# GpSimd's adds of the exponentials in a two-layer attention and expert kernel: one instruction per key tile instead of one per head

## What is computed

```python
# layer 0: x += 0.5 * moe0(layernorm(x)); x += attention0(layernorm(x)), 32 heads of 32; x += 0.5 * moe0(...)
# layer 1: attention1, 16 heads of 64; then routed experts with a capacity
qkv = data @ W_qkv + b_qkv
scores = jnp.einsum('nqhd,nkhd->nhqk', q, k)
attention = jax.nn.softmax(scores / jnp.sqrt(jnp.float32(HD)), axis=3)
out = jnp.einsum('nhql,nlhd->nqhd', attention, v).reshape(n, l, DIM)
return out @ W_out + b_out
# the router of layer 1: softmax over 8 experts, the two best, their weights divided by their sum
probs = jax.nn.softmax(xf @ router_w.T, axis=-1)
topw, topi = jax.lax.top_k(probs, K)
topw = topw / (topw.sum(-1, keepdims=True) + 1e-06)
```

## Time and profile before

| | us |
|---|---|
| median of three runs | 3018.5 |
| lowest and highest | 3016.71, 3020.96 |
| profiled execution: span from its first to its last instruction | 3025.9 |
| TensorE busy / share | 2770.4 / 92% |
| VectorE busy / share | 2107.9 / 70% |
| ScalarE busy / share | 1731.9 / 57% |
| GpSimd busy / share | 1752.1 / 58% |
| of it line 1982, 1152 adds | 1447.0 |

### The profile page before, as it was taken

How to read it: one execution, slowest core, us unless ns; L and a number is a source line. 1 busy time by engine, 2 the same in 40 slices (tenths; PEclk the granted TensorE clock), 3 DMA queues, 4 the chain that set the end, 5 groups by cost and what they waited for, 6 DMA issues and landing times. The chain is left out here.

```text
span 3025.9 us, 50008 instructions
## 1 busy us (share of the span) xinstructions
PE 2770.4 (92%) x17716; PEld 1938.1 (64%) x17716; DVE 2107.9 (70%) x4508; ACT 1731.9 (57%) x3340; POOL 1752.1 (58%) x1540
## 2 busy tenths in 40 slices
PE   7999999999999999989994787999999999999376
PEld 6995565656656565648883674666666666665276
DVE  5667777777777777666776435877877778777632
ACT  5665777776776767676772343544544545445142
POOL 0004989898898989891110573555555555555067
PEclk9999999999999999989996798999999999999588
DMA  3015444444544545420002331000000000000033
GB/s 101 1 58 129 119 117 117 115 114 109 130 106 113 123 106 131 105 71 5 23 15 67 72 60 33 2 5 5 9 5 6 5 9 5 5 6 9 28 84 50
DMA packets 146695, 179.65 MB, mean 59 GB/s; under 512 B 31571, under 2 KB 76176, under 8 KB 145936
## 3 DMA queue, kind: packets, MB, share of 16 engines
q1 hardware_dynamic: 132368, 165.72, 21.7%
q0 software_dynamic: 14080, 10.73, 2.7%
HBM read 56.51 MB, written 17.72 MB: 25 GB/s over the span
## 5 line engine op out<-in xcount | busy, mean ns | idle before, releaser
L1982 POOL TENSOR_TENSOR arena<-arena 128x512 f32<-128x512 f32 x1152 | 1447.0, 1284 | 565.7 <-ACT arena L1325 450.8
L1605 DVE TENSOR_REDUCE top<-psum 128x1 f32<-128x512 f32 x1536 | 974.6, 677 | 196.0 <-PE psum L917 123.6
L1325 ACT ACTIVATE arena<-psum 128x512 f32<-128x512 f32 x1536 | 840.8, 600 | 240.7 <-PE psum L917 141.3
L909 PE MATMUL psum<-stack 96*128 96x512 f32 (+1 forms) x2048 | 627.5, 426 | 16.5 <-ACT arena L1325 9.3
L960 PE MATMUL psum<-arena,values 128*32 128x512 f32 (+1 forms) x3072 | 477.6, 597 | 3.4 <-ACT arena L1325 3.4
L909 PEld LDWEIGHTS psum<-stack 96*128 96x128 f32 (+1 forms) x2048 | 344.0, 191 | 198.1 <-DVE top L1605 87.7
L960 PEld LDWEIGHTS psum<-arena,values 128*32 128x32 f32 (+1 forms) x3072 | 134.0, 119 | 290.0 <-issue 284.8
L917 PE MATMUL psum<-stack 64*128 64x512 f32 x2048 | 292.5, 399 | 11.8 <-DVE top L1605 5.6
L1951 POOL TENSOR_SCALAR rstd<-mv 128x4 f32<-128x4 f32 x56 | 13.0, 233 | 480.0 <-DVE mv L1466 478.1
L1636 DVE RECIPROCAL psum<-psum 128x128 f32<-128x128 f32 x256 | 228.5, 934 | 25.3 <-PE psum L999 25.3
L917 PEld LDWEIGHTS psum<-stack 64*128 64x128 f32 x2048 | 200.4, 184 | 59.0 <-issue 26.0
(11 more groups left out here) (189 smaller groups left out, 3895.3 us busy)
## 6 DMA issues: line engine op xcount, KB each, us to landing
stack<-halves SPq DMA_DIRECT2D x768, 128.0 KB, 2.3
qk_ring<-qk_split SPq DMA_DIRECT2D x64, 256.0 KB, 2.9
v_ring<-v_split SPq DMA_DIRECT2D x32, 256.0 KB, 3.0
tokens<-xn SPq DMA_DIRECT2D x16, 256.0 KB, 2.4
arena<-in_wg SPq DMA_DIRECT2D x16, 256.0 KB
arena<-in_wu SPq DMA_DIRECT2D x16, 256.0 KB
arena<-in_wd SPq DMA_DIRECT2D x16, 256.0 KB
wqkv<-in_w_qkv SPq DMA_DIRECT2D x2, 1536.0 KB, 9.5
```

What stands on the lines that cost most here:

```text
L909: return T_.matmul(bk, st[0:k, side, h, cols], st[0:k, 1 - side, h, :], start=True, stop=True)
L1325: S_.activation(prob[l][tile % N_PROB[l]][:, h, :], psum[:, bank[key], :], ACT.Exp, scale=scale).then_inc(released[bank[key]], 1)
L1605: give(V_.reduce_max(top[i][:, column:column + 1], psum[:, bank[key], :], AX.X), key)
L1982: ins = G_.tensor_tensor(to[:, h, :], old[:, h, :], prob[l][tile % N_PROB[l]][:, h, :], ALU.add)
```

## The change

GpSimd's loop over the heads goes, and one instruction over all heads of the tile stands in its place:

```diff
                             pool.wait_ge(*arena_free(l))
-                        for h in range(heads):
-                            ins = G_.tensor_tensor(to[:, h, :], old[:, h, :], prob[l][tile % N_PROB[l]][:, h, :], ALU.add)
-                        ins.then_inc(summed, 1)
+                        G_.tensor_tensor(to, old, prob[l][tile % N_PROB[l]], ALU.add).then_inc(summed, 1)
                     yield
```

## The result

The changed kernel takes 3030.24 us in the median of four runs (3029.06 to 3031.37), the kernel before beside it 3018.86 (3016.71 to 3020.96). The ratio is 1.0042, 95% interval 1.0027 to 1.0056: the medians lie 11.4 us apart, where 16.5 were forecast.

What follows compares the result with a forecast made beforehand. TensorE, busy 92%, sets the pace, with VectorE late where GpSimd's adds block it. Terms 6.5 + 10.6 - 0.6 + 0 = +16.5 us on the median 3018.5 gave 3035.0 us, range 3017 to 3040.

Steps and rivals of the forecast that it cites:

- Size of the adds: GpSimd's merged adds: 2.36 us for 128x1024 and 4.52 us for 128x2048, GpSimd busy 148 us less.
- Step 1: Second layer, line 1492: waits for the end of a longer add, +1.08 us six times, 6.5 us.
- Step 2: Second layer, line 1761: held by the third merged add, +1.9 us, 1.8 reaching TensorE, six times 10.6 us; otherwise -0.4.
- Second layer's end: Last three adds of the second layer, for which TensorE waits: shorter by 3 x 0.19, -0.6 us.
- Step 3: End of the first layer, line 1503 beside the adds: taken as 0, ends -2.2 and +4.5 us.
- The sum: All terms together: 6.5 + 10.6 - 0.6 + 0 = +16.5 us.
- one-for-one step: Second layer, behind line 1492: a further delay of VectorE goes to TensorE one for one.
- Rival (B): Line 1492 waits 1.08 us longer, line 1761 gets in before the third add: +5.3 us, 3024; chance 0.24.
- Rival (C): VectorE's delay doesn't grow, as GpSimd lets it in within a merged add: only -0.6 us, 3018; chance 0.21.
- Rival (D): Both VectorE lines stop being blocked, as GpSimd is idle between three adds: faster, 3011 us; chance 0.06.

Runs made afterwards that it cites:

- second profile of the change: The whole change run again, against the kernel before: median 3031.0 us, ratio 1.0047.
- first two sets: Follow-up kernels timed together in two sets, in which the kernel before took 3016.8 and 3016.6 us.
- The kernels without line 1492's wait: The change and the kernel before, each with line 1492 replaced by a one-input reduction: 3011.1 and 3021.6 us, both 0.9982 of the kernel before.
- the change with the ranks earlier: The whole change with VectorE's rank steps planned a fifth of a group earlier: 3046.6 us, 1.0061 of the kernel before.
- the kernel before with the ranks earlier: The kernel before with VectorE's rank steps planned a fifth of a group earlier: 3030.3 us, 1.0010 of the kernel before.

## Why the prediction came out as it did

**Size of the adds.** 2.36 and 4.52 us were worked out, 2.371 and 4.589 measured; the larger came out 1.5% above. GpSimd saved 110.7 us where 148 were predicted. The old side of the difference was 21 us too large: line 1982 counts 1.256 us of busy time an instruction (1447.0 / 1152), not 1.274. The new side was 15 us too small, nearly all of it in the larger add. So a merged pair saves 2.51 - 2.37 = 0.14 us and a merged four 5.02 - 4.59 = 0.43, and 192 x 0.57 = 110. On the path it made no difference.

**Step 1, line 1492.** +1.08 us predicted, 1435 to 2524 ns measured, +1.09; group 15.0 to 16.06 to 16.10 in the four batches at full clock; TensorE's wait 0.77 to 1.83. Right, and one for one. The kernel with kt 1 alone merged gives the same 16.1.

**Step 2, line 1761.** It was predicted 0.07 us behind the third add, and stood 0.08 behind in the sixth batch; 2.5 us predicted, 2.32 measured. The term was too large by a little: +1.73 against +1.9, and 1.60 of it in the next group (15.27 against 13.67) where 1.8 and 15.5 were forecast. The 2.5 counted 0.19 us of the instruction's own time behind the add's end; it ended 0.05 us behind it. One reading of the trace before was off without weight: line 1761 began 0.54 us before the end of an old add (0.73 us into one of 1.27), not 0.4.

**Second layer's end.** -0.6 predicted; TensorE's wait fell from 2.89 to 2.47, -0.4.

**Step 3, first layer's end.** Taken at 0 with ends -2.2 and +4.5. The four instructions of line 1503 take 3.64 us where they took 5.20, and TensorE's wait falls from 3.10 to 1.78. That fall isn't steady: the wait is 2.57 with the first layer alone merged and 2.56 in the second profile of the change. Steadier is the time from the layer's last line 948 to the end of both of TensorE's waits there (the second, for line 1162, falls from 0.85 to 0.42 us): 28.84 us before, 27.88 after, and 27.89 or 27.90 in five other profiles with this layer merged. So the end is 1.0 us shorter. Two profiles of unmerged kernels have 29.7 and one merged 28.7; the gain between them is the same. The reason I gave was off: the first two adds run in one row, 1346.56 to 1355.79, so line 1503 waits 1.2 us for the rest of the second and not 3.0.

**The sum.** Steps 1 and 2 were to lengthen the layer by 6.5 + 10.6 = 17.1 us; it is 16.8 longer. The two ends give -0.4 and -1.0, so the profile adds up to some 15.4. The measured ratio stands for 12.7 us [8.2, 16.9] and, measured a second time, for 14.2 [10.0, 18.1]. Both intervals hold 15.4 and the forecast's 16.5, but both centres lie below. Some of that may be the first layer, by the two differences of 2.4 and 2.7 us above. The profiles point there too: in the first two sets the stretch from the last line 948 of the first layer to the first one of the second takes 502.8 to 504.9 us in the four kernels with the first layer merged and 505.8 to 507.3 in the four without. That is more than the 1.0 us of the layer's end; what shortens the rest, in the experts, stays open.

The forecast was right in the place and the mechanism: both lines and the one-for-one step. That line 1761 would be held was a choice between +1.9 and -0.4 on a lead of 0.07 us, which no row of the kernel before showed to be enough; that it came right is in part luck. That the time lies in the range says little, since 3017 to 3040 also holds a kernel that doesn't change at all.

Rival (B) had the right place and the wrong outcome: 0.07 to 0.08 us were enough for the add to hold VectorE out, in the four batches at full clock. In the other two line 1761 came 0.44 and 0.67 us behind the add, and was held too. Rival (C) fell with the first 2524 ns. Rival (D) did not happen: both lines were held longer. The kernels without line 1492's wait show what it would have been worth: 0.9982 with merged adds, and the same 0.9982 without.

## What to carry to other kernels

Before lengthening an instruction of an engine off the critical path, look for what is blocked beside it: in the second layer the longer adds saved GpSimd 27 us (192 x 0.14) that nobody waited for, and made two instructions of VectorE, six times each, wait 1.1 and 1.7 us longer where TensorE stood behind them. The sign can be read from the trace of the kernel before: compare an instruction's longest time with its shortest (line 1492: 1453 and 390 ns; its median of 415 hides the six), see what the other engine does beside the slow ones, and take what is left of the longer instruction as the price. When a blocked instruction is moved, work out where every step behind it lands too.

## What the runs showed of the hardware

- The wait lasts to the end of GpSimd's instruction under way, whatever its length: line 1492, 0.42 us alone, takes 0.88 beside 128x256 adds, 1.44 beside 128x512 and 2.52 beside 128x1024, having started 0.13 to 0.14 us behind the add. It ends at a border between two of GpSimd's instructions even where they follow each other without a gap. The Trainium skill (SBUF — State Buffer, § Who interferes with whom) says that the one that comes second is blocked for the whole instruction of the other; all three lengths agree.
- A lead of 0.06 to 0.08 us in the records was enough for the add, in line 1761 (the change, four batches) and in line 1768 (the change with the ranks earlier, all six).
- An instruction with a single input in SBUF can be held too: line 1768, a TENSOR_SCALAR of 128x4, took 2.31 us when it began 0.07 us behind the start of a 128x1024 add, 0.63 when it began 0.67 us behind that of a 128x512 one, and 0.15 alone. I had looked at two-input instructions only. The same section of the Trainium skill names `tensor_scalar` among the operations that can enter a mode that takes the shared ports, if their operands meet its conditions, and `tensor_reduce` as one that never contends on this chip; the reduction of line 1495 ran its 0.40 us inside an add. Not every instruction with one input is held: the reciprocal of line 1751, 128x4, began 0.65 us into a 128x512 add in the kernel before with the ranks earlier and took 0.18 us, 0.17 alone.
- In two of the six batches TensorE's granted clock fell to 0.50, 1.2 GHz, right behind a wait of 1.83 us for VectorE; behind the same wait in the other four it did not. The other three kernels with kt 1 merged and line 1492 in its place show such groups of 17.6 to 17.7 us in two, three and one of the six batches, the kernels with shorter waits in none, nor does the one whose longest wait is 1.60 us. What tells the batches apart, no run here shows.
